# Graph attention over gathered neighbours: where each node's running sum is scaled and summed

## The chip, the cores and the metric

The kernel runs on one core of a Trainium2 chip. That core has five instruction streams that run side by side and meet at semaphores: TensorE (PE, matrix products into PSUM), VectorE (DVE), ScalarE (ACT), GpSimd (POOL), and SyncE (SP, which here only issues transfers). In the views, PEld is TensorE's own stream of weight loads. The metric is the device time of one execution in microseconds (us). Three executions of the kernel before took 4303.62, 4304.79 and 4323.05 us, so the median is 4304.79 us.

## The reference, cut to what matters

There are 12,500 nodes with 256 features and 200,000 edges. Queries, keys and values are projections of the nodes; a softmax over the edges of each node weighs the values of its neighbours; the result is projected again, added to the input and normalised.

```python
s = jnp.einsum('edh,edh->eh', q[row], k[col])            # one score per edge and head (8 heads of 32)
m = jax.ops.segment_max(s, row, num_segments=N)
e = jnp.exp(s - m[row])
z = jax.ops.segment_sum(e, row, num_segments=N)
out = jax.ops.segment_sum((e / z[row])[:, None, :] * v[col], row, num_segments=N)
x = _layernorm(x + out.reshape(N, -1) @ Wo.T + bo)
```

## The kernel before

The program has three parts. `prepare` sorts the edges by node, orders the nodes by their number of edges, and projects keys and values to rows in HBM. `one_round` walks over the edges. `finish` divides by the sum of weights, projects and normalises. The change lies in `one_round`.

`one_round` holds 98 tiles of 128 nodes, and one tile of padding, in an accumulator `acc` in SBUF: 264 numbers per node (8 heads of 32 values and one sum of weights). Beside it `runmax` holds each node's running maximum per head. The work is cut in 598 steps. A step belongs to one tile and treats three edges ("slots") of each of its 128 nodes. The order of the tiles is computed on the chip into a table, `step_tab`; steps beyond the real ones belong to the padding tile.

In a step k the engines do this:

- POOL issues three indirect transfers (L915), one per slot, each bringing 128 rows of keys and values of 520 numbers into `kv`. There are six buffers of `kv`, so POOL can be up to six steps ahead; it waits (`ready`, L902) until a buffer's values have been used.
- SP loads the tile's 128 queries (L936).
- DVE multiplies keys by queries (`score`, L790) and sums over each head (`score_sum`, L797), copies the old maximum beside the scores and adds the mask (`mask_scores`, L802 and L805), takes the new maximum (`maxima`, L812), and subtracts it (`differences`, L818). ACT makes the exponentials (`weights`, L961). The fourth column of weights is the factor by which the old sum must be scaled.
- DVE multiplies the values of two slots by their weights into the buffer `pv` (`weigh`, L825), ACT those of the third (`weigh_last`, L971, eight instructions). DVE scales the tile's old accumulator into a fourth place of `pv` (`carry`, L833).
- TensorE adds the four places with the identity as weights (`total`): two matrix products at L1025, then the scaled accumulator at L1027, then the third slot at L1029. In the trace each of these products is two instructions.
- ACT copies the sum from PSUM back into `acc` (`store`, L980).

There is no planner: each engine's order is written out by hand, in loops that are unrolled six steps. In DVE's stream the parts of three steps are interleaved: `score_sum` of step k+1, `weigh` of step k, `mask_scores` of k+1, `carry` of k, `maxima` of k+1, `score` of k+2, `differences` of k+1. `carry` of step k waits for `acc_stored`, that is for ACT's `store` of step k-1, because the next step may belong to the same tile. `store` waits for `summed`, TensorE's last product of the step. ACT's stream has `indices` (three row numbers for POOL), `weights` of k+1, `store` of k, `weigh_last` of k+1.

Of the kernel before, what the change touches and what calls it, by code (L numbers as in the profile page):

```python
# [12 lines left out]
P = 128  # L13
N, D, E = 12500, 256, 200000
HEADS = 8
HD = D // HEADS
# [22 lines left out]
G = 3  # L39
# [4 lines left out]
U = 6  # L44
# [627 lines left out]
def one_round(nc, new_sem, kv_rows, edge_keys, q_perm, ident, ones, upper, node_id, start_f, tile_deg,  # L672
# [8 lines left out]
    with ExitStack() as ps:  # L681
# [3 lines left out]
        def pp(name, shape, dtype=F32):  # L685
# [12 lines left out]
        pv = sb("pv", [P, 2, (G + 1) * VW])  # L698

        room = pv[:, :, :].rearrange("p b w -> p (b w)")  # L700
        step_f, past, tile_f = room[:, 0:STEPS], room[:, STEPS:2 * STEPS], room[0:1, 2 * STEPS:3 * STEPS]
# [12 lines left out]
        exp_made, pv_made, last_made, carry_made, summed, acc_stored = (  # L714
            sem(x) for x in ("exp_made", "pv_made", "last_made", "carry_made", "summed", "acc_stored"))
# [4 lines left out]
        with nc.Block() as block:  # L720

            @block.vector
            def _(dve):
# [116 lines left out]
                tile_r = [dve.alloc_register(f"tile_{b}") for b in range(2)]  # L840
                col_r = [dve.alloc_register(f"col_{b}") for b in range(2)]

                def look_up(k, b):
                    v = dve.value_load(step_tab[0:1, bass.ds(k, 1)], min_val=0, max_val=TAB * C * P - 1)
                    dve.reg_mov(tile_r[b], v & (P - 1))
                    dve.reg_mov(col_r[b], v >> PBITS)

                def step(k, j, turn, peel=False, last=False):
# [5 lines left out]
                    tile, tile1, col1 = bounded(dve, tile_r[b], TILES), bounded(dve, tile_r[b1], TILES), bounded(dve, col_r[b1], TAB * C - G)  # L854
                    look_up(k + 2, b)
# [25 lines left out]
                carry(k, k % 2, bounded(dve, tile_r[k % 2], TILES))  # L881
# [66 lines left out]
            def _(act):  # L948
# [26 lines left out]
                def store(k, b):  # L975

# [240 lines left out]
```

## Time and profile before

| what | value |
|---|---|
| median of three executions | 4304.79 us |
| span of the profiled execution, first to last instruction | 4998.2 us |
| busy share of that span: PE, DVE, ACT, POOL | 90%, 58%, 32%, 59% |
| instructions of one step: PE, POOL gathers | 8, 3 |

The profile comes from one execution of its own, with the span given; the page has no other time for that execution, and it is 693.4 us longer than the median of the timed ones. The stretches of the program are read off a table by stretch: from 0 to about 1400 us `prepare`, then the set-up of `one_round`, from about 1724 to 4440 us its steady steps, to about 4640 us steps of the padding tile, and from 4665 us `finish`.

### The profile page before, as it was taken

The page shows a single profiled execution, that of the slowest core. Times are in us where ns is not written, and L with a number is a line of the kernel's source. Part 1 is how long each engine was busy: PE and PEld are TensorE (multiplying, and loading weights), DVE is VectorE, ACT ScalarE, POOL GpSimd, SP SyncE. Part 2 cuts the span into 40 slices and gives each one's busy share as a digit, 9 for nine tenths or more (in the row PEclk, how much of TensorE's full clock was granted, in tenths as well). Part 3 has the DMA queues.
Part 4 walks back from the last instruction along what each step waited for, and adds up shares of the span by engine and source line. Part 5 has one row for each costly group of instructions (what it writes and reads, how often), then busy time and mean ns, then how long its engine had stood idle before and what let it go on. Part 6 is the DMA issues. An engine that isn't in the chain of part 4 may idle for free. (4 is left out here: it accounts for less than half of the span.)

```text
span 4998.2 us, 63175 instructions
## 1 busy us (share of the span) xinstructions
PE 4506.0 (90%) x8305; PEld 2637.9 (53%) x8305; DVE 2920.3 (58%) x7566; ACT 1624.4 (32%) x7078; POOL 2933.3 (59%) x2365
## 2 busy tenths in 40 slices
PE   4999999977810299999999999999999999999998
PEld 4567774333300155555555555555555555554565
DVE  6541454345461366666666666666666666666666
ACT  0100000111100144444444444444444444444322
POOL 2221120000076688888888888888888888886465
DMA  0100011111252366666666666666666666689222
GB/s 27 51 30 26 30 34 55 53 45 43 47 157 73 94 189 187 190 189 189 190 189 189 189 190 189 189 190 188 189 190 189 190 189 190 189 184 178 75 80 74
DMA packets 329217, 665.86 MB, mean 133 GB/s; under 512 B 63462, under 2 KB 191750, under 8 KB 329016
## 3 DMA queue, kind: packets, MB, share of 16 engines
q0 software_dynamic: 160768, 518.27, 38.1%
q1 hardware_dynamic: 168392, 146.96, 10.3%
q8 instruction: 20, 0.33, 0.0%
q14 instruction: 37, 0.30, 0.0%
HBM read 599.35 MB, written 65.86 MB: 133 GB/s over the span
## 5 line engine op out<-in xcount | busy, mean ns | idle before, releaser
L915 POOL DMA_INDIRECT kv<-kv_rows,idx x1794 | 2362.2, 1317 | 587.3 <-issue 560.8
L1025 PE MATMUL sum_ps<-pv,ident 128*128 128x264 f32 x2392 | 1612.1, 852 | 151.9 <-issue 146.7
L1025 PEld LDWEIGHTS sum_ps<-pv,ident 128*128 128x128 f32 x2392 | 847.4, 356 | 776.7 <-issue 606.5
L971 ACT ACTIVATE pv<-kv,s 128x33 f32<-128x33 f32 x4784 | 1081.1, 314 | 1.4 <-issue 1.4
L1029 PE MATMUL sum_ps<-pv,ident 128*128 128x264 f32 x1196 | 879.7, 857 | 0.1
L1027 PE MATMUL sum_ps<-pv,ident 128*128 128x264 f32 x1196 | 876.8, 854 | 1.9 <-issue 1.9
L833 DVE TENSOR_TENSOR pv<-acc,s 128x264 f32<-128x264 f32 x598 | 260.3, 435 | 876.1 <-ACT acc L980 782.5
L980 ACT ACTIVATE acc<-sum_ps 128x264 f32 x598 | 234.2, 392 | 1517.9 <-PE sum_ps L1029 1467.4
L797 DVE TENSOR_REDUCE s<-prod 128x24 f32<-128x768 f32 x598 | 569.9, 953 | 75.2 <-ACT pv L971 0.6
L1029 PEld LDWEIGHTS sum_ps<-pv,ident 128*128 128x128 f32 x1196 | 434.7, 364 | 300.9 <-issue 299.9
L790 DVE TENSOR_TENSOR prod<-kv,q 128x768 f32<-128x768 f32 x598 | 567.8, 950 | 42.9 <-DMA kv<-kv_rows,idx 41.4
L1027 PEld LDWEIGHTS sum_ps<-pv,ident 128*128 128x128 f32 x1196 | 428.6, 359 | 308.9 <-issue 272.9
L492 POOL DMA_INDIRECT kv_st<-node_rows,node_id x98 | 103.7, 1058 | 767.3 <-issue 749.8
L518 PE MATMUL kv_ps<-w_sb,xt_sb 128*128 128x512 f32 x392 | 489.3, 1425 | 0.0
L472 POOL TENSOR_SCALAR hot_hi<-hi_b 125x320 bf16<-125x320 bf16 x140 | 149.9, 1074 | 500.9 <-PE hist_ps L507 480.0
L507 PE MATMUL hist_ps<-hot_lo,hot_hi 125*98 125x128 bf16 x1600 | 371.9, 408 | 68.8 <-DVE hot_hi L174 68.8
L825 DVE TENSOR_TENSOR pv<-kv,s 128x528 f32<-128x528 f32 x598 | 417.9, 699 | 9.9 <-issue 9.0
L507 PEld LDWEIGHTS hist_ps<-hot_lo,hot_hi 125*98 125x98 bf16 x1600 | 371.3, 259 | 70.6 <-issue 70.5
L575 ACT ACTIVATE kv_st<-kv_ps 128x256 f32<-128x256 f32 x98 | 37.7, 385 | 1015.4 <-PE q_ps L519 1015.4
L172 DVE TENSOR_SCALAR hot_lo<-lo_b 125x320 bf16<-125x320 bf16 x640 | 164.3, 336 | 329.6 <-PE hist_ps L507 329.6
L518 PE MATMUL q_ps<-w_sb,xt_sb 128*128 128x256 f32 x392 | 257.6, 830 | 0.0
L1139 PE MATMUL y_ps<-wo_sb,oT 128*128 128x256 f32 x392 | 257.1, 836 | 0.0
(166 smaller groups left out, 3035.6 us busy)
## 6 DMA issues: line engine op xcount, KB each, us to landing
q<-q_perm SPq DMA_DIRECT2D x598, 128.0 KB
kv<-kv_rows,idx POOLq DMA_INDIRECT x1794
kv_rows<-kv_st SPq DMA_DIRECT2D x98, 260.0 KB, 2.3
xt_sb<-in_xT SPq DMA_DIRECT2D x98, 128.0 KB, 2.5
node_rows<-q_st SPq DMA_DIRECT2D x98, 128.0 KB, 2.6
q_perm<-kv_st SPq DMA_DIRECT2D x98, 128.0 KB
kv_st<-node_rows,node_id POOLq DMA_INDIRECT x98
cols<-edge_keys,run_at POOLq DMA_INDIRECT x98
```

Of the source, the lines that this page charges most:

```text
L507: last = pe.matmul(hist_ps[0:TILES, 0:P], hot_hi[:, :, e], hot_lo[:, :, e], start=c == 0 and e == 0, stop=c == CHUNKS - 1 and e == CH - 1)
L518: pe.matmul(ps[:, 0:b - a], xt_sb[:, j, kc, :], w_sb[:, kc, a:b], start=kc == 0, stop=False)
L790: dve.tensor_tensor(prod[:, :, :], kv[:, j, :, 0:D], q[:, j, :].unsqueeze(1).to_broadcast([P, G, D]), ALU.mult).then_inc(prod_made, 1)
L797: dve.tensor_reduce(s[:, b, 0:G * HEADS], prod[:, :, :].rearrange("p g (h d) -> p (g h) d", d=HD), AX.X, ALU.add).then_inc(scored, 1)
L825: dve.tensor_tensor(pv[:, b, 0:V * VW].rearrange("p (g h w) -> p g h w", g=V, w=HD + 1), kv[:, j, 0:V, D:KVW].rearrange("p g (h w) -> p g ...
L833: dve.tensor_tensor(pv[:, b, G * VW:].rearrange("p (h w) -> p h w", w=HD + 1), acc[:, bass.ds(tile * VW, VW)].rearrange("p (h w) -> p h w" ...
L915: pool.indirect_dma_start(out=kv[:, j, g, :], out_offset=None, in_=kv_rows, in_offset=bass.IndirectOffsetOnAxis(ap=idx[:, j, g:g + 1], axi ...
L971: last = act.activation(pv[:, b, V * VW + at_h:V * VW + at_h + HD + 1], kv[:, j, V, D + at_h:D + at_h + HD + 1], ACT.Copy, scale=s[:, b, V ...
L1025: pe.matmul(sum_ps[b][:, 0:VW], ident[:, :], pv[:, b, g * VW:(g + 1) * VW], start=g == 0, stop=False)
L1027: pe.matmul(sum_ps[b][:, 0:VW], ident[:, :], pv[:, b, G * VW:], start=False, stop=False)
L1029: pe.matmul(sum_ps[b][:, 0:VW], ident[:, :], pv[:, b, V * VW:G * VW], start=False, stop=True).then_inc(summed, 1)
L1139: pe.matmul(y_ps[h][:, 0:D], oT[:, h, kc * P:(kc + 1) * P], wo_sb[:, kc, :], start=kc == 0, stop=False)
```

## The change

DVE scales `acc` in place (`scale_acc`, L836 of the new file) instead of writing the scaled copy into `pv`, and later adds TensorE's sum of the three slots to it (`add_sum`, L844). TensorE's third product (the accumulator) and ACT's `store` are gone, and `pv` has three places instead of four. `add_sum` of step k-1 stands in DVE's stream of step k behind `maxima`; `scale_acc` of step k stands behind `score` of step k+2 and waits for that `add_sum`. TensorE's first product of a step waits for the `add_sum` two steps earlier, which has read the same PSUM buffer. DVE keeps three tiles' numbers in registers instead of two. A scratch row of the set-up, `tile_f`, moves from `pv` to `kv`, and the first six steps of TensorE stand ahead of its loop.

```diff
-        pv = sb("pv", [P, 2, (G + 1) * VW])
+        pv = sb("pv", [P, 2, G * VW])
...
-                def carry(k, b, tile, first=False):
+                def scale_acc(k, b, tile, first=False):
+
                     if not first:
-                        dve.wait_ge(acc_stored, k)
-                    dve.tensor_tensor(pv[:, b, G * VW:].rearrange("p (h w) -> p h w", w=HD + 1),
-                                      acc[:, bass.ds(tile * VW, VW)].rearrange("p (h w) -> p h w", w=HD + 1),
-                                      s[:, b, G * HEADS:].unsqueeze(2).to_broadcast([P, HEADS, HD + 1]), ALU.mult).then_inc(carry_made, 1)
+                        dve.wait_ge(acc_added, k)
+                    dve.wait_ge(exp_made, k + 1)
+                    at_tile = acc[:, bass.ds(tile * VW, VW)].rearrange("p (h w) -> p h w", w=HD + 1)
+                    dve.tensor_tensor(at_tile, at_tile,
+                                      s[:, b, G * HEADS:].unsqueeze(2).to_broadcast([P, HEADS, HD + 1]), ALU.mult).then_inc(acc_scaled, 1)
+
+                def add_sum(k, b, tile):
+
+                    dve.wait_ge(acc_scaled, k + 1)
+                    dve.wait_ge(summed, k + 1)
+                    at_tile = acc[:, bass.ds(tile * VW, VW)]
+                    dve.tensor_tensor(at_tile, at_tile, sum_ps[b][:, 0:VW], ALU.add).then_inc(acc_added, 1)
...
                     mask_scores(k + 1, b1, col1, tile1)
-                    carry(k, b, tile, first=peel and j == 0)
                     maxima(k + 1, b1, tile1)
+                    if before is not None:
+                        add_sum(k - 1, b1, before)
                     if not last:
                         score(k + 2, (j + 2) % U, turn + (j + 2) // U)
+                    scale_acc(k, b, tile, first=peel and j == 0)
                     differences(k + 1, b1, tile1)
...
-                def store(k, b):
-
-                    v = act.value_load(step_tab[0:1, bass.ds(k, 1)], min_val=0, max_val=TAB * C * P - 1)
-                    tile = bounded(act, v & (P - 1), TILES)
-                    act.wait_ge(summed, k + 1)
-                    act.activation(acc[:, bass.ds(tile * VW, VW)], sum_ps[b][:, 0:VW], ACT.Copy).then_inc(acc_stored, 1)
-
...
-                def total(k, b):
+                def total(k, b, peeled=False):
 
                     pe.wait_ge(pv_made, k + 1)
+                    if not peeled:
+                        pe.wait_ge(acc_added, k - 1)
                     for g in range(V):
                         pe.matmul(sum_ps[b][:, 0:VW], ident[:, :], pv[:, b, g * VW:(g + 1) * VW], start=g == 0, stop=False)
-                    pe.wait_ge(carry_made, k + 1)
-                    pe.matmul(sum_ps[b][:, 0:VW], ident[:, :], pv[:, b, G * VW:], start=False, stop=False)
                     pe.wait_ge(last_made, k + 1)
                     pe.matmul(sum_ps[b][:, 0:VW], ident[:, :], pv[:, b, V * VW:G * VW], start=False, stop=True).then_inc(summed, 1)
```

TensorE's stream of one step in the loop, before the change (`pv_made`, `carry_made` and `last_made` count what DVE's `weigh`, DVE's `carry` and ACT's `weigh_last` have written):

```order
L1025 MATMUL sum_ps<-pv,ident 128x264 [waits pv_made]
L1025 MATMUL sum_ps<-pv,ident 128x264
L1027 MATMUL sum_ps<-pv,ident 128x264 [waits carry_made]
L1029 MATMUL sum_ps<-pv,ident 128x264 [waits last_made]
L1023 REGISTER_ALU
```

The same place in the changed kernel, from the head of the loop:

```order
L1030 REGISTER_ALU [waits pv_made]
L1032 MATMUL sum_ps<-pv,ident 128x264 [waits acc_added]
L1032 MATMUL sum_ps<-pv,ident 128x264
L1034 MATMUL sum_ps<-pv,ident 128x264 [waits last_made]
L1028 REGISTER_ALU
L1032 MATMUL sum_ps<-pv,ident 128x264 [waits acc_added,pv_made]
```

Three products are left of four, and the wait inside the step for the scaled accumulator has become a wait at its head for an addition of two steps earlier.

DVE's stream in a step of the loop before, from the copy of the old maximum on (ISA rows are register work; `acc_stored` counts ACT's `store`):

```order
L802 COPY s<-runmax 128x8
L805 ISA [waits scored]
L805 TENSOR_TENSOR s<-s,mask 128x24
L833 ISA [waits acc_stored]
L833 TENSOR_TENSOR pv<-acc,s 128x264
L812 TENSOR_REDUCE runmax<-s 128x8 [waits masked,old_copied,tab_ready]
L790 TENSOR_TENSOR prod<-kv,q 128x768 [waits q_in3,kv_in3]
L818 TENSOR_TENSOR s<-s,runmax 128x32 [waits max_made]
```

The same place of the changed kernel (`summed` counts TensorE's steps, `acc_added` the additions of L844):

```order
L802 COPY s<-runmax 128x8
L805 ISA [waits scored]
L805 TENSOR_TENSOR s<-s,mask 128x24
L812 TENSOR_REDUCE runmax<-s 128x8 [waits masked,old_copied,tab_ready]
L844 ISA [waits summed,acc_scaled]
L844 TENSOR_TENSOR acc<-acc,sum_ps 128x264
L790 TENSOR_TENSOR prod<-kv,q 128x768 [waits q_in3,kv_in3]
L836 ISA [waits exp_made,acc_added]
L836 TENSOR_TENSOR acc<-acc,s 128x264
L818 TENSOR_TENSOR s<-s,runmax 128x32 [waits max_made]
```

One instruction of 264 columns has become two, the wait on ACT has become a wait on TensorE, and `maxima` stands ahead of it.

## Rows read from the trace of the kernel before

**Rows 1.** Span and mean granted TensorE clock.

```profile
core 0: 4998.2 us, clock 1.000
```

**Rows 2.** Stretches: length, busy PE, PEld, DVE, ACT, POOL, granted clock, DMA share, GB/s.

```profile
100.00:300.00 200.00, 200.00 (x569) 141.80 (x568) 71.50 (x222) 12.53 (x37) 29.02 (x28) 1.00 0.09 32
300.00:600.00 300.00, 300.00 (x804) 203.34 (x803) 125.09 (x428) 18.74 (x60) 58.06 (x56) 1.00 0.10 36
600.00:900.00 300.00, 295.57 (x679) 177.06 (x678) 129.46 (x345) 24.29 (x75) 29.05 (x28) 1.00 0.12 43
900.00:1400.00 500.00, 399.53 (x620) 172.32 (x618) 243.94 (x514) 67.45 (x173) 16.37 (x16) 1.00 0.19 50
1724.00:4440.00 2716.00, 2716.00 (x4424) 1592.06 (x4423) 1808.71 (x4423) 1287.61 (x6079) 2198.26 (x1658) 1.00 0.67 189
4440.00:4640.00 200.00, 196.80 (x314) 102.49 (x313) 131.72 (x312) 93.34 (x429) 141.25 (x115) 1.00 0.97 177
4665.00:4998.00 333.00, 319.47 (x681) 193.51 (x679) 217.79 (x872) 90.63 (x146) 198.67 (x194) 1.00 0.24 77
```

**Rows 3.** Waits, 2200 to 4400 us: total us, times, longest us.

```profile
ACT acc L980 <- PE sum_ps L1029: 1139.0, 441, 2.7
DVE pv L833 <- ACT acc L980: 600.7, 397, 1.6
POOL kv L915 <- issue: 416.8, 1344, 0.8
```

**Rows 4.** Timeline of PEld and PE around the step at 3000 us: start, us.

```profile
3004.59 0.28 PEld L1025 LDWEIGHTS sum_ps<-pv,ident 128*128 128x128 f32 x1 [0.36 <-DVE pv L825]
3005.08 2.81 PE L1025 MATMUL sum_ps<-pv,ident 128*128 128x264 f32 x4
```

**Rows 5.** Timeline of POOL, the same step.

```profile
3000.76 1.00 POOL L915 DMA_INDIRECT kv<-kv_rows,idx  x1 [0.30 <-issue]
3002.06 1.47 POOL L915 DMA_INDIRECT kv<-kv_rows,idx  x1 [0.30 <-issue]
3003.84 1.50 POOL L915 DMA_INDIRECT kv<-kv_rows,idx  x1 [0.30 <-issue]
```

**Rows 6.** Timeline of DVE, the same step.

```profile
3001.24 0.43 DVE L833 TENSOR_TENSOR pv<-acc,s 128x264 f32<-128x264 f32 x1 [1.50 <-ACT acc L980]
3001.59 0.20 DVE L812 TENSOR_REDUCE runmax<-s 128x32 f32 x1
3001.70 0.95 DVE L790 TENSOR_TENSOR prod<-kv,q 128x768 f32<-128x768 f32 x1
3003.76 0.70 DVE L825 TENSOR_TENSOR pv<-kv,s 128x528 f32<-128x528 f32 x1
```

**Rows 7.** Timeline of POOL when the steps begin.

```profile
1688.82 1.00 POOL L915 DMA_INDIRECT kv<-kv_rows,idx  x1 [5.71 <-ACT idx L957]
1690.12 1.00 POOL L915 DMA_INDIRECT kv<-kv_rows,idx  x1 [0.30 <-issue]
```

**Rows 8.** Timeline of DVE in a step of the padding tile.

```profile
4559.09 0.95 DVE L797 TENSOR_REDUCE s<-prod 128x24 f32<-128x768 f32 x1
4559.96 0.70 DVE L825 TENSOR_TENSOR pv<-kv,s 128x528 f32<-128x528 f32 x1
4561.00 0.43 DVE L833 TENSOR_TENSOR pv<-acc,s 128x264 f32<-128x264 f32 x1
4561.35 0.20 DVE L812 TENSOR_REDUCE runmax<-s 128x32 f32 x1
4563.41 0.96 DVE L790 TENSOR_TENSOR prod<-kv,q 128x768 f32<-128x768 f32 x1 [1.86 <-DMA kv<-kv_rows,idx]
4564.40 0.95 DVE L797 TENSOR_REDUCE s<-prod 128x24 f32<-128x768 f32 x1
```

**Rows 9.** DVE's addition from PSUM in `finish`: ns min/median/max.

```profile
L1098 DVE TENSOR_TENSOR y<-y_ps,x x98: 418/425/426, 4667.0 to 4985.1; 128x256 f32<-128x256 f32 x98
```

More of the change, by code:

```diff
@@ L697, in one_round @@
         s = sb("s", [P, 2, (G + 1) * HEADS])
[L698 removed]
+        pv = sb("pv", [P, 2, G * VW])
         room = pv[:, :, :].rearrange("p b w -> p (b w)")
[L701 removed]
+        step_f, past, tile_f = room[:, 0:STEPS], room[:, STEPS:2 * STEPS], kv[0:1, U - 1, :, :].rearrange("p g w -> p (g w)")[:, 0:STEPS]
         place_f = prod[0:1, :, :].rearrange("p g d -> p (g d)")[:, 0:STEPS]
@@ L713, in one_round @@
             sem(x) for x in ("prod_made", "scored", "old_copied", "masked", "max_made", "diffs_made"))
-        exp_made, pv_made, last_made, carry_made, summed, acc_stored = (
-            sem(x) for x in ("exp_made", "pv_made", "last_made", "carry_made", "summed", "acc_stored"))
+        exp_made, pv_made, last_made, acc_scaled, summed, acc_added = (
+            sem(x) for x in ("exp_made", "pv_made", "last_made", "acc_scaled", "summed", "acc_added"))
         CUT = 512
@@ L852, in step @@
                     weigh(k, j % U, b, peeled=peel and j < 2)
-                    tile, tile1, col1 = bounded(dve, tile_r[b], TILES), bounded(dve, tile_r[b1], TILES), bounded(dve, col_r[b1], TAB * C - G)
-                    look_up(k + 2, b)
+                    tile, tile1, col1 = (bounded(dve, tile_r[j % 3], TILES), bounded(dve, tile_r[(j + 1) % 3], TILES),
+                                         bounded(dve, col_r[(j + 1) % 3], TAB * C - G))
+                    before = None if peel and j == 0 else bounded(dve, tile_r[(j + 2) % 3], TILES)
+                    look_up(k + 2, (j + 2) % 3)
                     mask_scores(k + 1, b1, col1, tile1)
-                    carry(k, b, tile, first=peel and j == 0)
                     maxima(k + 1, b1, tile1)
+                    if before is not None:
+                        add_sum(k - 1, b1, before)
                     if not last:
                         score(k + 2, (j + 2) % U, turn + (j + 2) // U)
+                    scale_acc(k, b, tile, first=peel and j == 0)
                     differences(k + 1, b1, tile1)
@@ L880, in _ @@
                 weigh(k, k % U, k % 2)
-                carry(k, k % 2, bounded(dve, tile_r[k % 2], TILES))
+                tile, before = bounded(dve, tile_r[k % 3], TILES), bounded(dve, tile_r[(k - 1) % 3], TILES)
+                add_sum(k - 1, (k - 1) % 2, before)
+                scale_acc(k, k % 2, tile)
+                add_sum(k, k % 2, tile)
                 for r in tile_r + col_r:
@@ L990, in _ @@
                     weights(k + 1, (k + 1) % 2)
-                    store(k, k % 2)
                     weigh_last(k + 1, (k + 1) % U, (k + 1) // U, (k + 1) % 2, peeled=k == 0)
@@ L997, in _ @@
                         weights(k + 1, (j + 1) % 2)
-                        store(k, j % 2)
                         weigh_last(k + 1, (j + 1) % U, kk * (B // U) + (j + 1) // U, (j + 1) % 2)
@@ L1003, in _ @@
                     weights(k + 1, (k + 1) % 2)
-                    store(k, k % 2)
                     weigh_last(k + 1, (k + 1) % U, (k + 1) // U, (k + 1) % 2)
-                store(STEPS - 1, (STEPS - 1) % 2)
             @block.tensor
@@ L1019, in _ @@
                 last.then_inc(counts_made, 1)
-                def total(k, b):
+                def total(k, b, peeled=False):
                     pe.wait_ge(pv_made, k + 1)
+                    if not peeled:
+                        pe.wait_ge(acc_added, k - 1)
                     for g in range(V):
                         pe.matmul(sum_ps[b][:, 0:VW], ident[:, :], pv[:, b, g * VW:(g + 1) * VW], start=g == 0, stop=False)
-                    pe.wait_ge(carry_made, k + 1)
-                    pe.matmul(sum_ps[b][:, 0:VW], ident[:, :], pv[:, b, G * VW:], start=False, stop=False)
                     pe.wait_ge(last_made, k + 1)
                     pe.matmul(sum_ps[b][:, 0:VW], ident[:, :], pv[:, b, V * VW:G * VW], start=False, stop=True).then_inc(summed, 1)
-                with pe.Fori(0, LOOPS) as kk:
+                for j in range(B):
+                    total(j, j % 2, peeled=j < 2)
+                with pe.Fori(1, LOOPS) as kk:
                     for j in range(B):
```

10 lines of the change are left out of this document (5 added, 5 removed).

## The prediction

> **What bounds the kernel now.** I read the views in this order: span, stretches, waits, and then one step as a timeline.
>
> The span is 4998.2 us at a granted clock of 1.000, the 2.4 GHz level [rows 1]. The stretch table says where it goes. From 1724 to 4440 us TensorE is busy for all 2716 us with 4424 instructions [rows 2]; at 8 a step these are 553 steps of 2716/553 = 4.91 us, and one instruction takes 4.91/8 = 0.614 us. DVE is busy for 1809 us there and ACT for 1288 us. From 4440 us on the DMA share is 0.97 instead of 0.67: the steps of the padding tile are bound by transfers, and I expect nothing there. `prepare` between 100 and 900 us and `finish` are filled by TensorE too [rows 2].
>
> The waits agree. ACT's `store` waits for TensorE's last product (1139 us in this view), and DVE's `carry` waits for that `store` (600.7 us, up to 1.6 us each) [rows 3]. In the timeline DVE stands still for 1.50 us before `carry` [rows 6]. POOL is never released by another engine, it only has its own 0.30 us between gathers [rows 3, 5]. So in the profiled execution TensorE's pace sets the step, through a ring: last product, `store`, `carry`, third product.
>
> POOL is close behind. Alone, one gather follows the other after 1.30 us [rows 7], which makes 3 x 1.30 = 3.90 us a step. In the steady step two of three gathers take 1.47 and 1.50 us instead of 1.00 [rows 5]. Both end 0.88 us after a DVE multiplication that ran when they began: L790 ends at 3001.70 + 0.95 = 3002.65 and the gather at 3003.53; L825 ends at 3004.46 and the gather at 3005.34 [rows 5, 6]. So POOL has been held, and has 4.91 us in which this costs nothing.
>
> **The profiled execution against the timed ones.** The span is 693 us above the median of 4304.79 us. What bounds the profile must run faster when timed, and that is TensorE's pace, since TensorE fills most of the span. If the 693 us come off the stretches that TensorE fills (800 + 2716 + 333 = 3849 us), they are 18% of it; with 900 to 1400 us as well, 16% of 4349 us [rows 2]. The timed step is then 0.82 to 0.84 of 4.91 us, 4.03 to 4.12; I take 4.08 us. It can't be read directly; if the whole 693 us lay in these steps, the step would be 3.66 us, below POOL's 3.90 us.
>
> **The change part by part.**
>
> TensorE loses 2 of 8 instructions a step: 2 x 0.614 = 1.23 us at the profile's pace, which leaves 6 x 0.614 = 3.68 us. At the timed pace (0.83) that is 3.06 us.
>
> ACT loses `store` and its wait, 553 times. It was waiting for 1139 us in rows 3, so its own time saved is worth nothing by itself; what is worth something is that `weigh_last` no longer stands behind the end of the previous sum.
>
> DVE loses nothing and gains one addition with one input in PSUM. The nearest row is the addition of `finish`, 0.425 us for 256 columns [rows 9]; `carry` with 264 columns lasts 0.43 us, and the next instruction starts 0.35 us behind it [rows 8]. I take 0.35 us. From below the cost is nothing, if it fits in a stall; from above it is 0.43 us plus whatever wait it has. DVE's own chain without stalls is read from a step of the padding tile: L797 to L825 0.87, to L833 1.04, to L812 0.35 us, then 0.11 us to L790 [rows 6] and 0.99 us to the next L797 [rows 8], in all 3.36 us. With the addition it is 3.71 us. `scale_acc` is `carry` at another place and costs the same.
>
> The new wait: `add_sum` of step k-1 waits for TensorE's sum, and behind it on DVE are queued `score`, `scale_acc`, `differences`, and through these the exponentials of ACT and the next `weigh`. At the profile's pace `weigh` ends at 3004.46 [rows 6], the first product starts at 3005.08 [rows 4], six instructions take 5 x 0.614 plus 0.97 for the last (2.81 - 3 x 0.614, rows 4), so the sum is there 4.66 us after `weigh`, some 4.8 us with a semaphore. From there DVE needs 0.35 + 0.99 + 0.35 + 0.87 + 0.70 = 3.26 us to the end of the `weigh` of the step after next [rows 8]. The ring takes two steps, so it asks for (4.8 + 3.26)/2 = 4.03 us a step. At the timed pace the first part is about 0.83 x 4.8 = 4.0 us, and the ring asks for 3.6 us.
>
> The other wait, TensorE for `add_sum` of two steps earlier, costs nothing: that addition is done before the `weigh` for which TensorE waits anyway. The moves of `tile_f` and of six steps ahead of the loop act once. At the very end two additions and one sum stand where `carry`, a sum and `store` stood: between nothing and 2 us, I take 0.
>
> The sum for the profile: limits of 3.68 (TensorE), 3.71 (DVE), 3.90 (POOL), 4.03 us (the ring); 553 x (4.91 - 4.03) = 487 us, so a span near 4510 us. The sum for the timed execution: limits of 3.06, 3.71, 3.90 and 3.6 us. POOL is last. 553 x (4.08 - 3.90) = 100 us less than 4304.79 us: 4205 us. Most of what the profile will show as gained has been gained already in the timed execution by the faster TensorE.
>
> **Where the skill bears on it.** Held gathers: the Trainium skill (SBUF — State Buffer, "SBUF: two separate sides") says that DVE and GpSimd share a pair of ports as an exclusive lock, taken by a DVE operation with two SBUF inputs against a GpSimd operation that reads SBUF, and that the loser waits to its end. The 0.88 us above agree. By that rule `add_sum`, with one input in PSUM, takes no lock, and the locks of a step stay what they were; it speaks against the change in one way, that DVE's stall of 1.50 us, in which a gather ran at 1.00 us, goes away.
>
> **The rivals.**
>
> The gathers are held more often (slower). With a step of 3.90 us and a chain of 3.71 us DVE hardly rests, and L790, `scale_acc` and L818 follow one another. For it: two of three gathers are held now [rows 5], at 0.47 and 0.50 us. Against it: three gathers of 1.30 us can lie so that the one that is held ends with L790 and the two others begin outside a multiplication. If one gather in each step pays 0.47 us, the step is 3.90 + 0.47 = 4.37 us and the time 4305 + 553 x 0.29 = 4465 us. It decides from 0.18 us a step on, where the gain is used up.
>
> POOL was the bound already in the timed execution (no change). For it: 4.08 is near 3.90 us, and 0.18 us of holding would fill the difference. Against it: then `prepare` and `finish` must have given up less than their share, or POOL held as much as the profile shows. The time stays at about 4305 us.
> The Trainium skill (TensorE: Matmul & The Clock Gate, "Back-to-back issue gap") puts a product of 264 columns at 264/2.4 + 2.5 = 112 ns for a pass at 2.4 GHz; the trace has 614 ns for an instruction at a granted clock of 1.000, and no run here shows the page's pace. By it TensorE would be no bound at all when timed, which is this rival.
>
> Everything runs faster when timed (more gain). If the profile slows POOL and DVE as it slows TensorE, the ratio of the profiles holds: 4304.79 x 4510/4998 = 3885 us. Against it: a gather of 1.00 us and its 0.30 us repeat to 0.01 us wherever POOL is alone [rows 7]. In between lies a POOL that is a little faster, with DVE's 3.71 us as the limit: 4305 - 553 x 0.37 = 4100 us.
>
> **How the numbers follow.** The forecast, 4205 us, has 0.46, with a range of its own from 4150 to 4270 us (553 steps that lose between 0.06 and 0.28 us). More gain has 0.12, no change 0.20, held gathers 0.22. A measurement of this kernel can tell about 0.5% from no change, 22 us. Faster is then 0.46 + 0.12 = 0.58, within 0.5% 0.20, slower 0.22. The range takes in half of more gain and half of the slower case: 4040 to 4420 us.
>
> **What would show it.** In the profile after, six TensorE instructions a step, a step of 4.0 to 4.1 us, no wait of DVE on ACT, a wait of DVE's addition on TensorE of some 0.3 us, and ACT waiting mostly for DVE. TensorE's pace should stay at 0.61 us an instruction. The addition should last 0.43 us with 0.35 us to the next instruction. The forecast is wrong in its mechanism if POOL shows waits for other engines, or if the span falls by 400 us or more and the timed execution falls as much; it is wrong in sign if gathers of 1.47 us and more come three a step.

## The result, and the profile after

The changed kernel takes 4030.02 us (median of 4 runs, 4015.67 to 4069.82) against 4308.73 us for the kernel before, measured beside it (4 runs, 4303.62 to 4323.05): a ratio of 0.9366, 95% interval 0.9315 to 0.9417. The gain is 279 us where 100 us were forecast, and the time lies below the forecast range of 4040 to 4420 us. When the changed kernel ran again (e11, e13), one execution of four was in a slower state each time (4105.74 and 4109.65 us), which the ratios leave out.

The span of the profiled execution after, beside [rows 1], and the one of a fresh profile of the kernel before, which was taken in the first experiment (e0) and is the one to compare with:

```profile
core 0: 4015.6 us, clock 0.743
```

```profile
core 0: 4341.1 us, clock 0.749
```

Rows 1 had 4998.2 us at a clock of 1.000. The fresh profile of the same kernel is 657 us shorter, and its execution was timed at 4343.1 us, 2 us more than its span; the first span lies 693 us above the timed median (4304.79 us). What follows compares after with this profile, and [rows 2 to 6] are shown to be of another pace.

The stretch table of the fresh profile of before (columns as in [rows 2]: length, busy PE, PEld, DVE, ACT, POOL, granted clock, DMA share, GB/s), in the set-up and in the middle of the steps:

```profile
300.00:600.00 300.00, 255.83 (x1043) 232.13 (x1044) 154.39 (x489) 14.97 (x48) 58.09 (x56) 0.58 0.10 30
1800.00:3400.00 1600.00, 1000.09 (x2793) 635.48 (x2792) 1189.15 (x2792) 841.81 (x3840) 1280.98 (x1048) 0.78 0.73 203
```

The same stretches after:

```profile
300.00:600.00 300.00, 254.85 (x1044) 231.82 (x1045) 154.08 (x488) 15.23 (x49) 58.02 (x56) 0.59 0.10 31
1800.00:3400.00 1600.00, 843.16 (x2394) 528.54 (x2393) 1497.64 (x3590) 852.17 (x3987) 1235.15 (x1197) 0.79 0.80 232
```

In the set-up, which the change does not touch, both run 1043 or 1044 TensorE instructions in 300 us, where [rows 2] show 804 for the same 300 us. In the steps, POOL's three gathers a step count them: 1048/3 = 349 steps in 1600 us before, 4.58 us each, and 399 after, 4.01 us each. 553 x (4.58 - 4.01) = 315 us, of the 325 us between the two spans. (The medians differ by 279 us: the profiled execution of before was 34 us slower than its median, that of after 12 us faster.) So the gain is in the steps. TensorE is busy for 63% of the time before and 53% after: it bounds neither. DVE goes from 74 to 94%.

The waits in that stretch (total us, times, longest us), first before, in the fresh profile:

```profile
DVE prod L790 <- DMA kv<-kv_rows,idx: 391.2, 336, 1.8
DVE pv L833 <- ACT acc L980: 2.1, 6, 0.6
```

and after:

```profile
PE sum_ps L1032 <- DVE pv L825: 757.1, 399, 2.5
ACT s L977 <- DVE s L818: 711.1, 399, 1.9
```

The wait on which the prediction rested, `carry` for ACT's `store`, 600.7 us in [rows 3], is 2.1 us in the fresh profile. There DVE waits for gathered rows instead, 1.12 us a step (391.2/349), and after the change it waits for nothing of size. The groups by line say what became of the gathers (operation and count | busy us, mean ns of one | idle before and its cause). Before:

```profile
L915 POOL DMA_INDIRECT kv<-kv_rows,idx x1048 | 1281.5, 1223 | 319.3 <-issue 317.5 <-ACT idx L957 1.5 <-ACT pv L971 0.3
L790 DVE TENSOR_TENSOR prod<-kv,q 128x768 f32<-128x768 f32 x349 | 334.8, 959 | 391.3 <-DMA kv<-kv_rows,idx 391.2
```

After:

```profile
L931 POOL DMA_INDIRECT kv<-kv_rows,idx x1197 | 1235.8, 1032 | 364.9 <-issue 364.9
L790 DVE TENSOR_TENSOR prod<-kv,q 128x768 f32<-128x768 f32 x399 | 379.5, 951 | 0.0
L844 DVE TENSOR_TENSOR acc<-acc,sum_ps 128x264 f32 x399 | 171.2, 429 | 14.1
L836 DVE TENSOR_TENSOR acc<-acc,s 128x264 f32 x399 | 170.1, 426 | 0.0
```

A gather takes 1.223 us before and 1.032 us after, plus the 0.30 us between two of them that [rows 7] show: 3 x (1.223 + 0.305) = 4.58 us, 3 x (1.032 + 0.305) = 4.01 us. POOL issues one gather behind the other in both kernels, and the whole difference of a step is in how long they last. This sum alone does not show that POOL sets the step. It holds for [rows 5] too (1.00 + 1.47 + 1.50 + 3 x 0.30 = 4.87 us), where DVE stood waiting for ACT, and for e6 below, where DVE's chain sets the step and the gathers are held for whatever time is left. The experiments decide.

One step of the fresh profile of before shows why (start, us, instruction, idle before it and its cause), DVE and POOL in one order of time:

```profile
2503.79 0.96 DVE L790 TENSOR_TENSOR prod<-kv,q 128x768 f32<-128x768 f32 x1 [1.49 <-DMA kv<-kv_rows,idx]
2503.90 1.72 POOL L915 DMA_INDIRECT kv<-kv_rows,idx  x1 [0.30 <-issue]
2505.65 0.70 DVE L825 TENSOR_TENSOR pv<-kv,s 128x528 f32<-128x528 f32 x1
2505.93 1.29 POOL L915 DMA_INDIRECT kv<-kv_rows,idx  x1 [0.30 <-issue]
2507.53 1.00 POOL L915 DMA_INDIRECT kv<-kv_rows,idx  x1 [0.30 <-issue]
2508.63 0.96 DVE L790 TENSOR_TENSOR prod<-kv,q 128x768 f32<-128x768 f32 x1 [1.40 <-DMA kv<-kv_rows,idx]
```

The first gather begins 0.11 us after L790 did, and ends 0.87 us after L790's end (2504.75 to 2505.62). The second begins under L825 and ends 0.87 us after its end (2506.35 to 2507.22). The third meets no multiplication and takes 1.00 us. From issue to landing the rows of a gather take 3.9 us (transfer, count, median us):

```profile
kv<-kv_rows,idx POOLq DMA_INDIRECT x1048, 3.9
```

So the L790 at 2508.63 doesn't wait for the two gathers ahead of it (begun at 2505.93 and 2507.53), which belong to the next step, but for the one held by the L790 before: its own step's third slot, begun at 2503.90. By the trace's semaphores the last of those rows landed at 2508.60, 2.98 us after the gather's end, and in that time POOL issues two more gathers and comes to the third slot of the next step, 0.20 us behind L790's start. That closes a cycle (not the prediction's ring): L790, held gather, landing, L790, with 0.96 + 0.87 + 2.98 + 0.03 = 4.84 us. This step takes 4.84 us; the mean of 4.58 us has steps in which the gathers are held for less.

After the change the same two engines read so:

```profile
2502.20 1.00 POOL L931 DMA_INDIRECT kv<-kv_rows,idx  x1 [0.30 <-issue]
2502.74 0.95 DVE L790 TENSOR_TENSOR prod<-kv,q 128x768 f32<-128x768 f32 x1
2503.50 1.06 POOL L931 DMA_INDIRECT kv<-kv_rows,idx  x1 [0.31 <-issue]
2504.87 1.00 POOL L931 DMA_INDIRECT kv<-kv_rows,idx  x1 [0.30 <-issue]
2504.92 0.70 DVE L825 TENSOR_TENSOR pv<-kv,s 128x528 f32<-128x528 f32 x1
```

DVE waits for nothing, so L790's start is no longer tied to a landing. (The gather that runs when L790 starts costs DVE nothing: the 399 L790 of this stretch all begin under one and last 0.951 us.) A gather begins 0.19 us before L790's end and is held for 0.06 us; the next begins 0.05 us ahead of L825 and is not held. Of the 399 gathers that begin under L790 in this stretch the mean is 1.102 us, and none begins under L825; before, 312 began under L790 (mean 1.448 us) and 337 under L825 (1.276 us).

### The profile page after: what moved, and what is told of

Read it like the earlier page. It is cut to its first block and busy times, and to the rows that moved or that the text cites. A ratio compares the mean times of both kernels' runs of the same rounds, so it can differ in the third digit from the quotient of the medians.

```text
span 4015.6 us, 59591 instructions
## 1 busy us (share of the span) xinstructions
PE 2227.2 (55%) x7109; PEld 1514.8 (38%) x7109; DVE 3211.0 (80%) x8164; ACT 1504.6 (37%) x6480; POOL 2447.6 (61%) x2365
## 5 line engine op out<-in xcount | busy, mean ns | idle before, releaser
L931 POOL DMA_INDIRECT kv<-kv_rows,idx x1794 | 1863.0, 1038 | 583.7 <-issue 538.5
L1032 PE MATMUL sum_ps<-pv,ident 128*128 128x264 f32 x2392 | 902.0, 512 | 1299.3 <-DVE pv L825 1299.3
L1032 PEld LDWEIGHTS sum_ps<-pv,ident 128*128 128x128 f32 x2392 | 511.3, 237 | 1712.1 <-DVE pv L825 1393.1
L790 DVE TENSOR_TENSOR prod<-kv,q 128x768 f32<-128x768 f32 x598 | 569.2, 952 | 59.7 <-DMA kv<-kv_rows,idx 59.6
L977 ACT ACTIVATE s<-s 128x32 f32<-128x32 f32 x598 | 137.0, 229 | 1126.1 <-DVE s L818 1126.1
L1034 PE MATMUL sum_ps<-pv,ident 128*128 128x264 f32 x1196 | 497.3, 508 | 0.0
L825 DVE TENSOR_TENSOR pv<-kv,s 128x528 f32<-128x528 f32 x598 | 417.4, 698 | 0.3 <-ACT s L977 0.3
L1034 PEld LDWEIGHTS sum_ps<-pv,ident 128*128 128x128 f32 x1196 | 296.6, 248 | 70.3 <-ACT pv L987 0.4
L844 DVE TENSOR_TENSOR acc<-acc,sum_ps 128x264 f32 x598 | 256.6, 429 | 22.2 <-PE sum_ps L1034 1.1
L836 DVE TENSOR_TENSOR acc<-acc,s 128x264 f32 x598 | 255.0, 426 | 0.3
L518 PE MATMUL kv_ps<-w_sb,xt_sb 128*128 128x512 f32 x392 | 200.5, 636 | 0.0
L812 DVE TENSOR_REDUCE runmax<-s 128x32 f32 x598 | 123.7, 207 | 79.3
L973 ACT ACTIVATE idx<-cols 128x3 int32 x598 | 113.2, 189 | 139.0 <-DVE round_base L782 136.6
L1178 POOL DMA_INDIRECT x<-in_x_rows,node_id x98 | 112.7, 1150 | 56.9 <-issue 30.7
```

The source lines that it names most:

```text
L518: pe.matmul(ps[:, 0:b - a], xt_sb[:, j, kc, :], w_sb[:, kc, a:b], start=kc == 0, stop=False)
L790: dve.tensor_tensor(prod[:, :, :], kv[:, j, :, 0:D], q[:, j, :].unsqueeze(1).to_broadcast([P, G, D]), ALU.mult).then_inc(prod_made, 1)
L825: dve.tensor_tensor(pv[:, b, 0:V * VW].rearrange("p (g h w) -> p g h w", g=V, w=HD + 1), kv[:, j, 0:V, D:KVW].rearrange("p g (h w) -> p g ...
L836: dve.tensor_tensor(at_tile, at_tile, s[:, b, G * HEADS:].unsqueeze(2).to_broadcast([P, HEADS, HD + 1]), ALU.mult).then_inc(acc_scaled, 1)
L844: dve.tensor_tensor(at_tile, at_tile, sum_ps[b][:, 0:VW], ALU.add).then_inc(acc_added, 1)
L931: pool.indirect_dma_start(out=kv[:, j, g, :], out_offset=None, in_=kv_rows, in_offset=bass.IndirectOffsetOnAxis(ap=idx[:, j, g:g + 1], axi ...
```

## The experiments

The theory: a gather that begins while DVE multiplies two operands that both lie in SBUF is held until the multiplication has ended. In the kernel before, DVE waits for gathered rows, and this wait puts L790, and L825 behind it, just where the next gathers begin. The change adds work to DVE's chain, and this makes the chain longer than POOL's three unheld gathers, so DVE stops waiting and the gathers slip between its multiplications. The rivals: TensorE's third product was the bound; the ring from the last product over `store` to `carry` was. Step lengths and means below are of 1800 to 3400 us; the number of steps there is in brackets. Time is the median, the ratio is to the kernel before measured beside it, with the 95% interval in brackets. e2, e3 and e4 leave out part of the sums, as said at each, and serve for their times alone.

**e0, the kernel before again.** No edit.

> The kernel before, unchanged, profiled once more. The profile of the changed kernel has a granted clock that goes up and down (mean 0.743) and TensorE instructions of 264 columns every 0.22 or 0.44 us; the profile that the prediction rests on has a constant 1.00 and one every 0.61 us, and is 693 us longer than the timed executions. Theory A (that profile was of another state of TensorE than the timed executions, and a fresh one will resemble the timed ones): a span near 4303 us, TensorE at 0.22 to 0.44 us an instruction, a step near 4.5 us ((4305 - 1274 - 295 - 240) / 553, with the other stretches as long as in the changed kernel). Theory B (the profile itself slows TensorE in this kernel): a span near 4998 us and 0.61 us an instruction again.

The time was 4343.1 us, and the step of 4.58 us is near theory A's 4.5; its rows stand above. The granted clock of 1.000 in the first profile came with slower products. In the first profile of before (first line) and in the fresh one (second line; ns min/median/max, stretch) the 512-column products of the set-up read:

```profile
L518 PE MATMUL kv_ps<-w_sb,xt_sb x392: 1257/1406/1542, 143.0 to 1351.9; 128*128 128x512 f32 x196
```

```profile
L518 PE MATMUL kv_ps<-w_sb,xt_sb x392: 590/592/1222, 143.0 to 926.6; 128*128 128x512 f32 x196
```

1406 ns against 592. The steps begin (first L825) at 1706 us in the first profile and at 1275 us in the fresh one: 431 of the 657 us lay ahead of all steps. The steps account for 553 x (4.91 - 4.58) = 182 us. What gave the first profiled execution its pace, no run settles.

**e2, no third product.** The old sums are lost; DVE and ACT do all they did.

```diff
-                    pe.matmul(sum_ps[b][:, 0:VW], ident[:, :], pv[:, b, G * VW:], start=False, stop=False)
```

> The kernel before without TensorE's third product (the scaled accumulator is made but not summed, so the old sums are lost). Everything else stays: ACT's store, DVE's carry, all waits. Theory H: no change within 1.5%, 4250 to 4370 us, gathers still of 1.2 us. Theory T: TensorE's load was what cost, so most of the gain comes, 4030 to 4120 us.

4341.18 us, ratio 1.0043 (1.0016 to 1.0069); step 4.56 us (351), gathers 1.217 us, DVE's wait for rows 388.7 us. A quarter of TensorE's products in a step is gone and nothing is gained.

**e3, no ring.** `carry` scales a constant tile and waits for no `store`.

```diff
-                    if not first:
-                        dve.wait_ge(acc_stored, k)
...
-                                      acc[:, bass.ds(tile * VW, VW)].rearrange("p (h w) -> p h w", w=HD + 1),
+                                      still[:, :].rearrange("p (h w) -> p h w", w=HD + 1),
```

> The kernel before with the ring cut: carry scales a constant tile instead of the accumulator and doesn't wait for ACT's store (the old sums are lost); four products, store and everything else stay. Theory H: no change within 1.5%, 4250 to 4370 us. Theory T: the ring last product, store, carry, third product was what cost, so most of the gain comes, 4030 to 4120 us.

4319.71 us, ratio 0.9986 (0.9952 to 1.002). The lines of its profile for gathers and L790 (here L792):

```profile
L792 DVE TENSOR_TENSOR prod<-kv,q 128x768 f32<-128x768 f32 x354 | 340.5, 962 | 426.7 <-DMA kv<-kv_rows,idx 426.3
L915 POOL DMA_INDIRECT kv<-kv_rows,idx x1062 | 1277.7, 1203 | 323.7 <-issue 321.0 <-ACT idx L957 2.4 <-ACT pv L971 0.3
```

The ring that the prediction called the bound is gone, DVE waits as long as ever for its rows (426.3/354 = 1.20 us a step), and the gathers stay held. Taken singly, both rivals fall; e4 and e5 below settle it for the two together.

**e1, e10 and e5, the kernel before with idle work on DVE.** Behind `maxima` DVE adds a constant PSUM tile to a constant SBUF tile, result unused, of 264 columns (e1), 384 (e10) and 512 (e5). Nothing is taken away.

```diff
+                def idle(k, first=False):
+                    if not first:
+                        dve.wait_ge(idle_made, k)
+                    dve.tensor_tensor(idle_out[:, :], idle_in[:, :], idle_ps[:, 0:VW], ALU.add).then_inc(idle_made, 1)
...
                     maxima(k + 1, b1, tile1)
+                    idle(k, first=peel and j == 0)
```

> The kernel before with one more DVE instruction in each step behind `maxima`: an addition of 264 columns with one input in PSUM, of constants, whose result nobody reads. Theory H (held gathers): in the kernel before, as profiled anew, POOL bounds the step at 3 x (1.22 + 0.31) = 4.6 us because DVE's multiplications hold its gathers, and DVE waits 1.1 us a step for data; with a DVE chain of about 3.8 us, close to POOL's unheld 3.9 us, DVE no longer waits, the gathers slip between the multiplications, and the kernel gets faster although it does more: gathers of 1.0 to 1.1 us, a step near 4.0 us, 4000 to 4080 us. Theory T (TensorE and the way over ACT): nothing is gained, 4300 us, or up to 4500 us if the 0.35 us comes on top.

> The kernel before with an idle DVE addition of 384 columns a step, between the 264 that gave 1% and the 512 that gave 7%. DVE's chain is then about 3.85 us, still under POOL's 3.92 us. If the gathers are held as long as DVE has to wait for data (a threshold at POOL's 3.92 us): little more than with 264 columns, 4220 to 4300 us. If the holding falls in proportion to the time that DVE waits: about halfway, 4130 to 4190 us.

> The kernel before with one more DVE addition in each step behind `maxima`, now of 512 columns (one input in PSUM, constants, nobody reads the result). With 264 columns DVE's chain was 3.73 us, still under POOL's unheld 3.92 us, DVE still waited 0.8 to 1.0 us for data, and 1% was gained. 248 columns more make the chain 3.98 us. Theory H2 (the gathers are held as long as DVE's chain is shorter than POOL's three unheld gathers, and slip past once it is longer): a jump, gathers of 1.0 to 1.1 us, a step of 4.0 to 4.05 us, 4000 to 4070 us, with four products, store and the ring all still there. Theory O (it is the order of DVE's instructions in the changed kernel, not the length of its chain): about what the 264 columns gave, 4250 to 4330 us.

e1 took 4289.51 us, ratio 0.9906 (0.9841 to 0.9971), step 4.49 us (356): far less than expected. Its chain (DVE's step without its wait for rows) measures 3.73 us, less than POOL's 3 x (1.00 + 0.305) = 3.92 us, so DVE still waits (lines of e1):

```profile
L795 DVE TENSOR_TENSOR prod<-kv,q 128x768 f32<-128x768 f32 x356 | 342.2, 961 | 240.8 <-DMA kv<-kv_rows,idx 239.9
L926 POOL DMA_INDIRECT kv<-kv_rows,idx x1068 | 1275.3, 1194 | 325.6 <-issue 321.0 <-ACT idx L968 3.0 <-ACT pv L982 1.5
```

e5, with a chain of 3.94 to 3.98 us, took 4025.59 us, ratio 0.9289 (0.9249 to 0.9328), step 4.00 us (400). Lines of e5:

```profile
L926 POOL DMA_INDIRECT kv<-kv_rows,idx x1201 | 1235.4, 1029 | 366.0 <-issue 359.3 <-ACT idx L968 6.7
L795 DVE TENSOR_TENSOR prod<-kv,q 128x768 f32<-128x768 f32 x400 | 380.4, 951 | 1.0 <-DMA kv<-kv_rows,idx 0.4
```

The kernel before, with useless work added and nothing removed, is as fast as the changed kernel. This is the strongest evidence here: adding to DVE is enough for the gain. That taking from TensorE and ACT is not enough, e4 shows below.

e10, with 3.80 to 3.85 us, took 4029.2 us, ratio 0.9313 (0.9289 to 0.9337), step 4.01 us, gathers 1.031 us. That was not expected: the theory put the turn at 3.92 us. DVE still waits for rows here, 29.2 us in 81 steps, and the mean of 25 steps in a row goes from 3.95 to 4.41 us. The turn lies between 3.73 and 3.80 to 3.85 us; why there, and not at 3.92, stays open.

**e4 and e6, the changed kernel with a shorter and a longer chain.** e4 scales and adds only 33 of 264 columns of the accumulator; e6 adds the idle work of e1. The core of e4's edit:

```diff
-                    at_tile = acc[:, bass.ds(tile * VW, VW)]
-                    dve.tensor_tensor(at_tile, at_tile, sum_ps[b][:, 0:VW], ALU.add).then_inc(acc_added, 1)
+                    at_tile = acc[:, bass.ds(tile * VW, HD + 1)]
+                    dve.tensor_tensor(at_tile, at_tile, sum_ps[b][:, 0:HD + 1], ALU.add).then_inc(acc_added, 1)
```

> The changed kernel with scale_acc and add_sum cut to one head of eight (33 of 264 columns; the other heads are neither scaled nor summed), so that DVE's chain is some 0.45 us shorter, 3.5 instead of 3.96 us. Theory H: POOL leads again, DVE waits for data, the gathers are held again (1.15 us or more), and the kernel gets slower with less work: a step of 4.3 us or more, 4180 to 4350 us. Plain theory (DVE's 3.96 us is the bound after the change, nothing else): the step falls to POOL's 3.92 us or below, 3950 to 4000 us.

> The changed kernel with the same idle DVE addition of 264 columns behind `maxima`. Theory H2: DVE bounds the changed kernel with 3.96 us and no held gather, so 0.35 us a step come on top in some 553 steps: a step of 4.3 to 4.4 us, 4190 to 4260 us. If POOL bounded it (its 3.92 us with little holding), part of the 0.35 us would be hidden: 4050 to 4150 us.

e4, with less work than the changed kernel and than the kernel before, took 4379.2 us, slower still than expected, ratio 1.0104 (1.0028 to 1.0181), step 4.66 us (343). Lines of e4:

```profile
L931 POOL DMA_INDIRECT kv<-kv_rows,idx x1031 | 1286.8, 1248 | 314.3 <-issue 262.7 <-ACT idx L973 51.5
L790 DVE TENSOR_TENSOR prod<-kv,q 128x768 f32<-128x768 f32 x343 | 329.1, 959 | 355.8 <-DMA kv<-kv_rows,idx 355.4
```

The wait for rows is back and the gathers are held again, with TensorE's and ACT's savings in place. e6 took 4163.63 us, ratio 0.9609 (0.9557 to 0.9661), step 4.27 us (375), a little under what was expected. DVE waits for no rows; the gathers under L790 (here L795; mean 1.352 us) are held for the time that DVE has more to do. Past the turn the chain sets the step, so among chains with both operands in SBUF the best is the shortest one that still keeps DVE from waiting.

**e7, the kernel before with `weigh`'s weights in PSUM.** ACT writes a second copy of the weights to PSUM and L825 (here L827) reads it there. Same number of DVE instructions; ACT has one more.

```diff
-                                      s[:, b, 0:V * HEADS].rearrange("p (g h) -> p g h", h=HEADS).unsqueeze(3).to_broadcast([P, V, HEADS, HD + 1]),
+                                      wt_ps[:, b, 0:V * HEADS].rearrange("p (g h) -> p g h", h=HEADS).unsqueeze(3).to_broadcast([P, V, HEADS, HD + 1]),
```

> The kernel before in which ACT writes the weights of two slots a second time, into PSUM, and DVE's `weigh` (L825) reads them there, so that this multiplication has one SBUF input instead of two; all else stays, with one more ACT instruction of 0.23 us. Theory H: a gather that begins under `weigh` is no longer held by it and takes 1.0 us; those under L790 still are; the mean falls from 1.22 to about 1.1 us, the step to 4.2 to 4.4 us, 4080 to 4220 us. If a held gather has another cause than DVE's second SBUF input: no change, 4290 to 4350 us.

4046.33 us, ratio 0.9339 (0.9288 to 0.9389), step 4.05 us (395), gathers 1.048 us: more gain than the 4080 to 4220 us expected. DVE and POOL in one order of time in its profile:

```profile
2504.22 0.69 DVE L827 TENSOR_TENSOR pv<-kv,wt_ps 128x528 f32<-128x528 f32 x1
2504.75 1.00 POOL L917 DMA_INDIRECT kv<-kv_rows,idx  x1 [0.30 <-issue]
```

The gather begins under L827 and is not held. All 336 that began under it took 994 to 1002 ns, where 337 under L825 had a mean of 1276 ns. Those under L790 (here L792), whose inputs are both in SBUF still, kept a mean of 1355 ns. In e5, 391 gathers began under the idle addition, which has one input in PSUM, and took 998 ns in the mean. A longer chain is not e7's reason: with ACT's extra instruction DVE stands 0.26 us a step before the copy of the old maximum instead of 0.05, which adds less than the addition of e1, and e1 gained 1%. So it is the place of the second operand that holds a gather, not that DVE is busy or writes. This agrees with the Trainium skill (SBUF — State Buffer, "Who interferes with whom"), by which a DVE instruction with two SBUF inputs contends with a GpSimd instruction that reads SBUF and one with at most one SBUF input, outside its 2-port performance modes, does not. The same section infers that generating descriptors is not stalled by such an instruction; here the issue of a gather that reads its row numbers from SBUF is. The prediction's sentence on the lock, by which the loser waits, agrees for POOL alone: L790 under a running gather is no longer (0.951 us, above).

**e9 and e12, both multiplications without a second SBUF input.** e7, and ACT also copies each step's queries to PSUM for L790. In e9 the copy stands behind ACT's `weigh_last`, in e12 right behind the exponentials:

```diff
                         weights(k + 1, (j + 1) % 2)
+                        move_q(k + 3, (j + 3) % U, kk * (B // U) + (j + 3) // U, (j + 3) % 2)
                         store(k, j % 2)
                         weigh_last(k + 1, (j + 1) % U, kk * (B // U) + (j + 1) // U, (j + 1) % 2)
-                        move_q(k + 3, (j + 3) % U, kk * (B // U) + (j + 3) // U, (j + 3) % 2)
```

> The kernel before with both large multiplications of DVE freed of their second SBUF input: `weigh` reads its weights from PSUM as in the last such run, and `score` reads the queries from PSUM, where ACT copies them (one more ACT instruction of 256 columns a step). Nothing is taken from TensorE, DVE or the ring. Theory H: no gather is held for longer than carry lasts (0.43 us), POOL sets the step with 3 x 1.31 = 3.92 us plus little, DVE's chain of 3.4 us is no bound: a step of 3.92 to 3.97 us and 3965 to 4020 us, a little under the changed kernel. If ACT, now busy for 3.2 us a step and with more waits, becomes the bound: 4030 us or more.

> As the run with both multiplications freed of their second SBUF input, but ACT copies the queries straight behind the exponentials instead of behind its eight multiplications, so that DVE's `score` no longer waits for that copy (it waited 0.84 us a step, and the step became 4.51 us with no gather held). Theory H: with no gather held and no new wait POOL's three gathers of 1.00 us and their 0.31 us are the bound: 3.92 us a step, perhaps 0.03 us at the loop's end, 3960 to 4010 us, below the changed kernel. If the step stays above 4.1 us with gathers of 1.00 us, something else than POOL and its holding bounds this kernel at a level above 3.92 us, and the account of the kernel before as bound by POOL is incomplete.

e9 took 4292.82 us, ratio 0.9923 (0.9907 to 0.994), step 4.51 us (355). Its gathers have a mean of 0.998 us, none held by the two large multiplications, and that bought almost nothing, against the 3965 to 4020 us expected, because two waits on ACT took the place (waits of e9; the copied queries lie in `tab_ps`):

```profile
DVE prod L793 <- ACT tab_ps L992: 297.3, 355, 0.9
POOL kv L918 <- ACT idx L960: 275.9, 318, 1.0
```

The copy is too late for L790, and ACT in turn comes late with the next row numbers. e12 takes this wait away: 3969.94 us, ratio 0.9174 (0.9152 to 0.9196), step 3.91 us (409). Its gathers, and DVE's wait for rows:

```profile
L918 POOL DMA_INDIRECT kv<-kv_rows,idx x1227 | 1226.8, 1000 | 374.1 <-issue 349.7 <-ACT idx L960 21.7 <-ACT pv L976 2.7
```

```profile
DVE prod L793 <- DMA kv<-kv_rows,idx: 93.5, 215, 1.1
```

This is POOL's limit of 3 x (1.000 + 0.305) = 3.92 us, met with DVE waiting, which costs nothing once its two large multiplications hold no gather (59 began under `carry`, with a mean of 1.041 us). It beats both kernels, the changed one by 1.4%, measured beside it (e13: 4027.18 us).

**e8, the changed kernel with twelve steps in a turn of the loop.** This was to take away DVE's longer step at the end of each turn of six.

```diff
-B = 6
+B = 12
```

> The changed kernel with its loops unrolled twelve steps instead of six. In the changed kernel every sixth step takes 4.21 instead of 3.96 us; if that 0.25 us belongs to the loop's end, half of it goes away: 46 x 0.25 = 12 us, 4000 to 4025 us. If it belongs to something with a period of six steps that isn't the loop (the six buffers), no change.

4277.22 us, ratio 0.9871 (0.9817 to 0.9926), not the small gain expected. From one L790 to the next, eleven steps of twelve take 3.96 to 4.35 us and one 9.24 to 10.15 us. In one of those DVE and POOL read:

```profile
2508.30 0.71 DVE L825 TENSOR_TENSOR pv<-kv,s 128x528 f32<-128x528 f32 x1 [2.17 <-issue]
2509.91 1.00 POOL L931 DMA_INDIRECT kv<-kv_rows,idx  x1 [4.48 <-DVE pv L825]
```

and the queue that loads instructions (packets, MB, share) in e8, then in the changed kernel:

```profile
q14 instruction: 280, 2.29, 0.2%
```

```profile
q14 instruction: 37, 0.30, 0.0%
```

DVE stands 2.17 us without a releaser, and 2.29 MB of instructions are loaded instead of 0.30, in the steps five packets for each turn of some 53 us: the longer turn is fetched again each time. The shorter one is not: from 1325 to 3693 us this queue of the changed kernel has no packet. The Trainium skill (Runtime: NRT & Kernel Launch, "Instruction fetch mechanics") gives a reason for such a stall that fits: a taken branch to instructions that are no longer held stops the engine for a fetch.

**e11 and e13, the changed kernel again,** beside e9 and e10, and beside e12.

> The changed kernel once more, on the chip of these runs, to compare with: 4015 to 4070 us, gathers of 1.03 us, a step of 4.01 us.

> The changed kernel on the same chip, to compare with: 4015 to 4070 us.

4024.52 us, ratio 0.9295 (0.9275 to 0.9314), and 4027.18 us, 0.9303 (0.9273 to 0.9332), gathers 1.032 and 1.033 us. The result repeats, with a slightly larger gain than at first.

## Why the prediction was right or wrong

**The sign was right, by luck.** The forecast had the gain come from TensorE's ring, given up to POOL's floor. It came from held gathers, and the price of the step before was wrong by 0.50 us, more than the 0.18 us of gain forecast. What made the kernel faster, DVE's longer chain, stood in the prediction as a cost. The step of 4.0 to 4.1 us that the profile was to show did come, 4.01, but from DVE's chain and not from the ring of 4.03.

**The step that failed: "What bounds the profile must run faster when timed, and that is TensorE's pace".** TensorE did run faster in an execution as short as the timed ones (592 instead of 1406 ns a product, e0), but the conclusion, a timed step of 4.03 to 4.12 us taken as 4.08, is where it breaks: it measured 4.58 us. The prediction spread the 693 us by share over all that TensorE filled; of the 657 us between the profiles 431 lay ahead of the steps and 182 in them. And a faster TensorE handed the steps to another bound, the held gathers, which the scaling could not see. In [rows 5] POOL was never idle for longer than 0.30 us; the prediction took its held time (0.97 us a step) as free to vanish, and in the step before 0.67 us of it stayed (3 x 0.223). With 4.58 in place of 4.08 and 4.01 in place of 3.90 the same sum gives 315 us.

**"POOL's 3.90 us is last" holds as a floor,** and nearly as the step after. e12 reaches 3.91. The changed kernel takes 4.01, since DVE's chain is longer than forecast: five steps of a turn take 3.97 us and the sixth 4.21.

**DVE's 3.71 us measured 3.96.** The changed kernel's step on DVE, beside [rows 8]:

```profile
2514.05 0.18 DVE L805 TENSOR_TENSOR s<-s,mask 128x24 f32<-128x24 f32 x1
2514.37 0.21 DVE L812 TENSOR_REDUCE runmax<-s 128x32 f32 x1
2514.59 0.43 DVE L844 TENSOR_TENSOR acc<-acc,sum_ps 128x264 f32 x1
2514.93 0.95 DVE L790 TENSOR_TENSOR prod<-kv,q 128x768 f32<-128x768 f32 x1
2515.80 0.42 DVE L836 TENSOR_TENSOR acc<-acc,s 128x264 f32 x1
2516.15 0.18 DVE L818 TENSOR_TENSOR s<-s,runmax 128x32 f32<-128x32 f32 x1
2516.25 0.94 DVE L797 TENSOR_REDUCE s<-prod 128x24 f32<-128x768 f32 x1
2517.11 0.70 DVE L825 TENSOR_TENSOR pv<-kv,s 128x528 f32<-128x528 f32 x1
2517.88 0.17 DVE L802 COPY s<-runmax 128x8 f32 x1
```

The addition lasts 0.43 us with 0.34 us to the next start, as forecast, and `scale_acc` costs 0.35. Missing was what `carry` had covered: L812 needs L805's result and now starts 0.32 us after it, where `carry` in between started 0.16 us after it (e1's trace: 2503.84 and 2504.00), and L844 starts 0.22 us after L812 where L790 needed 0.11. Together that is 0.27 us, about the 0.25 by which the chain is longer. Here the mis-sized term helped: e1's chain of 3.73 us, almost the one that was forecast, does not reach the turn.

**The new waits cost nothing, but not for the reason given.** `add_sum` was to wait 0.3 us for TensorE; it was idle for 14.1/399 = 0.04 us. TensorE's instructions were to stay at 0.61 us; in the changed kernel's step above they read:

```profile
2513.85 1.16 PE L1032 MATMUL sum_ps<-pv,ident 128*128 128x264 f32 x4 [2.36 <-DVE pv L825]
2514.84 0.61 PE L1034 MATMUL sum_ps<-pv,ident 128*128 128x264 f32 x2
```

Six take 1.60 us (2513.85 to 2515.45), so the ring of 4.03 or 3.6 us never came near.

**The rival of held gathers saw the mechanism with the wrong sign.** It argued that a DVE that hardly rests holds more gathers. The runs show the opposite: a DVE that waits for gathered rows multiplies at the very moment when the next gather begins, and in the changed kernel, where it runs through, it holds one gather a step, for 0.1 us. The 0.88 us of [rows 5, 6] were read rightly; not asked was what sets the phase between the two engines. **"POOL was the bound already"** was right on the bound, also on holding as what fills the difference, and drew the wrong conclusion, because its length of step was not fixed. **"Everything runs faster when timed"** forecast 4100 or 3885 us from POOL and DVE being faster; they are not (an unheld gather 1.00 us, L790 0.95 or 0.96 us, in the first profile and in every later one).

## What to carry to other kernels

Here an engine that waited for transfers started in step with the engine that issues them, and its instructions held that engine. Then work added to the first was worth more than work removed, and the cure was to take away the hold (an operand in PSUM, e12), not to tune the chain's length. An engine without idle time isn't yet the bound: ask whether its instructions are held by another. Where the span of a profile is far from the timed runs, take another profile before working out any step, since the two may have different bounds.

## What the runs showed of the hardware

- A gather that begins under a DVE multiplication with both inputs in SBUF ends 0.87 us after the multiplication's end, unless its 1.00 us last longer than that (it was up to 1.79 us long in the fresh profile of before). In e7 the 336 that began under the multiplication with one input in PSUM took 0.997 us.
- A gather that begins ahead of the multiplication isn't held: in the fresh profile of before none of the 248 that began up to 1 us ahead of L790 or L825 took longer than 1.03 us.
- The rows of a gather landed 3.9 us after its issue (median, fresh profile of before).
- The turn is sharp: 0.07 to 0.12 us more on DVE a step (e1 to e10) is worth 260 us.
- A granted clock of 1.000 did not mean a fast TensorE: 512-column products took 1406 ns at 1.000 in the first profile of before, and 592 ns in the fresh one, where the clock granted from 300 to 600 us is 0.58.
- Twelve steps in a turn of the loop cost a stop of some 5.8 us in every turn (9.77 us for that step, by the median, instead of 3.97) and 2 MB of instruction loads; with six, one step in a turn took 0.24 us longer and nothing was loaded in the steps.
